# The B and C terms of a selective scan: multiplied on other engines, the B term in place in PSUM

## What is computed

```python
A = -jnp.exp(A_log)
BandC = x @ W_bc.T + b_bc
Bm, Cm = (BandC[..., :n], BandC[..., n:])
delta = jax.nn.softplus(s1 @ W_d.T + b_d)
deltaA = jnp.exp(jnp.einsum('bld,dn->bldn', delta, A))
deltaB_u = jnp.einsum('bld,bln,bld->bldn', delta, Bm, x)
def step(h, inp):
    dA_i, dBu_i, c_i = inp
    h = dA_i * h + dBu_i
    y = jnp.einsum('bdn,bn->bd', h, c_i)
    return (h, y)
```

## Time and profile before

| what | us |
|---|---|
| median of three runs | 6350.38 |
| span of the profiled execution, first to last instruction | 6356.3 |
| TensorE matmul busy | 4749.8 (75%) |
| VectorE busy | 4716.0 (74%) |
| GpSimd busy | 3798.1 (60%) |
| ScalarE busy | 2523.2 (40%) |
| mean granted TensorE clock | 0.837 of full |

### The profile page before, as it was taken

The page is one execution under the profiler, slowest core; times in us unless marked ns, Lnnn a source line. Parts: engine busy times, 40 slices in busy tenths (PEclk is TensorE's granted clock), DMA queues, the critical chain, the costliest instruction groups (busy, mean ns, idle before and its releaser), DMA issues. The chain is left out here.

```text
span 6356.3 us, 78277 instructions
## 1 busy us (share of the span) xinstructions
PE 4749.8 (75%) x24156; PEld 3749.7 (59%) x24156; DVE 4716.0 (74%) x6611; ACT 2523.2 (40%) x4450; POOL 3798.1 (60%) x1772
## 2 busy tenths in 40 slices
PE   3557777777777777777777777777777888887887
PEld 3335555555555555555555555555567777777777
DVE  3899999889999998999899898999733333333333
ACT  2555445555554455555445555554301111111110
POOL 1876666667666666666666666666425555555554
PEclk7578888888788888888888888888988889888888
DMA  2000000000000000000000000000025555555554
GB/s 51 9 22 18 18 20 26 18 18 26 18 18 19 26 19 18 18 26 18 18 20 26 18 18 26 18 10 12 16 70 123 129 124 132 123 130 123 126 128 107
DMA packets 150308, 302.51 MB, mean 48 GB/s; under 512 B 22288, under 2 KB 97492, under 8 KB 149960
## 3 DMA queue, kind: packets, MB, share of 16 engines
q1 hardware_dynamic: 98680, 227.16, 12.7%
q0 software_dynamic: 49152, 69.84, 6.2%
q10 hardware_dynamic: 2128, 1.26, 0.1%
HBM read 236.39 MB, written 61.80 MB: 47 GB/s over the span
## 5 line engine op out<-in xcount | busy, mean ns | idle before, releaser
L476 POOL TENSOR_TENSOR state<-du,b_wide 128x972 f32<-128x972 f32 x512 | 1826.1, 3567 | 463.9 <-ACT b_wide L513 301.5
L610 DVE TENSOR_TENSOR_SCAN state<-decay,state 128x972 f32<-128x972 f32 x512 | 1718.6, 3357 | 81.6 <-POOL state L476 63.3
L486 POOL TENSOR_TENSOR y<-y,state 128x972 f32<-128x972 f32 x448 | 1063.3, 2373 | 962.2 <-DVE state L616 962.2
L513 ACT ACTIVATE b_wide<-ps 128x972 f32<-128x972 f32 x512 | 500.1, 977 | 1120.8 <-PE ps L785 1118.2
L774 PE MATMUL ps<-x2f,ws_u 128*116 128x324 f32 x1024 | 470.7, 547 | 432.5 <-DVE ag L759 431.6
L1072 PE MATMUL e_ps<-xgt,w_up 96*116 96x192 f32 x4096 | 734.4, 333 | 23.7 <-DVE e_ag L1045 23.5
L807 PE MATMUL ps<-ws_d,inter 116*98 116x192 f32 (+1 forms) x3072 | 642.5, 371 | 126.9 <-DVE h L621 124.7
L1072 PEld LDWEIGHTS e_ps<-xgt,w_up 96*116 96x116 f32 x4096 | 680.6, 184 | 27.7 <-DVE e_ag L1045 26.2
L807 PEld LDWEIGHTS ps<-ws_d,inter 116*98 116x98 f32 (+1 forms) x3072 | 585.2, 203 | 160.3 <-DVE h L621 140.2
L1030 DVE TENSOR_TENSOR passed<-counts,tk 96x648 f32<-96x648 f32 x128 | 106.2, 830 | 753.3 <-DMA counts<-running_counts,row_idx 753.3
L983 POOL DMA_INDIRECT xg<-token_rows,gather_idx x256 | 244.8, 956 | 644.0 <-DVE gather_idx L1041 594.5
(11 more groups left out here) (170 smaller groups left out, 8485.2 us busy)
## 6 DMA issues: line engine op xcount, KB each, us to landing
w_up<-in_we_up SPq DMA_DIRECT2D x128, 696.8 KB
w_down<-in_we_down SPq DMA_DIRECT2D x128, 348.0 KB
x_in<-in_x SPq DMA_DIRECT2D x32, 1176.0 KB, 5.3
running_counts<-cnt SPq DMA_DIRECT2D x32, 324.0 KB, 3.3
token_rows<-x SPq DMA_DIRECT2D x64, 148.5 KB
out_rows<-h SPq DMA_DIRECT2D x64, 147.0 KB
token_rows<-x SPq DMA_DIRECT2D x32, 194.0 KB
h<-in_txt SPq DMA_DIRECT2D x32, 192.0 KB, 2.6
```

The lines of the kernel that those rows point to most:

```text
L476: nc.gpsimd.tensor_tensor(b.state[n % 4][:], b.du[t.p][:], b.b_wide[n % 2][:], ALU.mult).then_inc(input_ready, 1)
L486: nc.gpsimd.tensor_tensor(y, y, b.state[n % 4][:], ALU.add).then_inc(y_added, 1)
L513: nc.scalar.activation(b.b_wide[k % 2][:].rearrange("p a t -> p (a t)"), flat[:, b_bank:b_bank + 3 * L], ACT.Copy).then_inc(b_copied, 1)
L610: nc.vector.tensor_tensor_scan(s, b.decay[k % 2][:].rearrange("p a t -> p (a t)"), s, 0.0, ALU.mult, ALU.add).then_inc(scan_done, 1)
```

## The change

B and C swap their ways. **B:** VectorE multiplies the B broadcast with `du` in place in PSUM (piece `fill_b`), and the scan reads its input there and writes `state`. **C:** ScalarE copies the C broadcast to SBUF (`c_wide`, in the place of `b_wide`), and GpSimd multiplies the state with it in place. GpSimd's add is a piece of its own, `add_y`. TensorE may refill `b_bank` once the scan before has ended (`scan_done`) in place of ScalarE's copy (`b_copied`), and `c_bank` once ScalarE has copied (`c_copied`) in place of VectorE's product (`c_used`). The wait that frees one of the four `state` tiles (`y_added`) goes from GpSimd to the scan. The positions of the pieces are new. B is no longer filled two states ahead, but just before its scan.

```diff
--- before.py
+++ after.py
...
 
@@ -74,14 +64,13 @@
 
     for n in range(N):
 
-        b, lag = 2 * (n - 2) + 1, 0
-        if b < 0:
-            b, lag = b + 32, -1
-        put("fill_b", lag, n, pe=b, act=b + 1, pool=b + 2)
+        b, lag = (2 * n - 1.1, 0) if n else (30.9, -1)
+        put("fill_b", lag, n, pe=b, dve=b + 0.9)
         d, lag = (2 * n - 1.5, 0) if n else (30.5, -1)
         put("decay", lag, n, act=d + 0.3)
         put("scan", 0, n, dve=2 * n)
-        put("fill_c", 0, n, pe=2 * n, dve=2 * n + 1.2, pool=2 * n + 2)
+        put("fill_c", 0, n, pe=2 * n - 0.4, act=2 * n + 0.5, pool=2 * n + 1.8)
+        put("add_y", 0, n, pool=2 * n + 2.7)
     for k in range(3):
...
                 for kind, lag, n in todo:
                     t = i.plus(-lag)
-                    if kind == "fill_b":
-
-                        if n == 0:
-                            pool.wait_ge(du_ready, t.v + 1)
-                        pool.wait_ge(b_copied, N * t.v + n + 1)
-                        wait(pool, y_added, 15 * t.v + (max(n - 4, 1) if n >= 4 else n - 3))
-                        nc.gpsimd.tensor_tensor(b.state[n % 4][:], b.du[t.p][:], b.b_wide[n % 2][:], ALU.mult).then_inc(input_ready, 1)
-                    elif kind == "fill_c" and n > 0:
+                    if kind == "fill_c":
+                        pool.wait_ge(c_copied, N * t.v + n + 1)
+                        pool.wait_ge(scan_done, N * t.v + n + 1)
+                        nc.gpsimd.tensor_tensor(b.state[n % 4][:], b.state[n % 4][:], b.c_wide[n % 2][:], ALU.mult).then_inc(c_used, 1)
+                    elif kind == "add_y" and n > 0:
 
                         pool.wait_ge(c_used, N * t.v + n + 1)
                         y = b.y[t.p][:]
@@ -507,10 +493,10 @@
                         to = b.decay[k % 2]
                         nc.scalar.activation(to[:, 0:2, 1:L], b.delta[t.p][:, 0:2, 1:L], ACT.Exp, scale=b.a_neg[:, 0, k:k + 1])
                         nc.scalar.activation(to[:, 2, 1:L], b.delta[t.p][:, 2, 1:L], ACT.Exp, scale=b.a_neg[:, 1, k:k + 1]).then_inc(decay_ready, 1)
-                    elif kind == "fill_b":
-                        act.wait_ge(b_full, N * t.v + k + 1)
-                        wait(act, input_ready, N * t.v + k - 1)
-                        nc.scalar.activation(b.b_wide[k % 2][:].rearrange("p a t -> p (a t)"), flat[:, b_bank:b_bank + 3 * L], ACT.Copy).then_inc(b_copied, 1)
+                    elif kind == "fill_c":
+                        act.wait_ge(c_full, N * t.v + k + 1)
+                        wait(act, c_used, N * t.v + k - 1)
+                        nc.scalar.activation(b.c_wide[k % 2][:].rearrange("p a t -> p (a t)"), flat[:, c_bank:c_bank + 3 * L], ACT.Copy).then_inc(c_copied, 1)
                     elif kind == "emb_a":
 
                         act.wait_ge(x_loaded, 16 * t.v + 16)
@@ -603,17 +589,19 @@
             def body(i, todo, use):
                 for kind, lag, k in todo:
                     t = i.plus(-lag)
-                    if kind == "scan":
+                    if kind == "fill_b":
+                        if k == 0:
+                            dve.wait_ge(du_ready, t.v + 1)
+                        dve.wait_ge(b_full, N * t.v + k + 1)
+                        into = flat[:, b_bank:b_bank + 3 * L]
+                        nc.vector.tensor_tensor(into, into, b.du[t.p][:].rearrange("p a t -> p (a t)"), ALU.mult).then_inc(input_ready, 1)
+                    elif kind == "scan":
                         dve.wait_ge(decay_ready, N * t.v + k + 1)
                         dve.wait_ge(input_ready, N * t.v + k + 1)
+                        wait(dve, y_added, 15 * t.v + (max(k - 4, 1) if k >= 4 else k - 3))
                         s = b.state[k % 4][:].rearrange("p a t -> p (a t)")
-                        nc.vector.tensor_tensor_scan(s, b.decay[k % 2][:].rearrange("p a t -> p (a t)"), s, 0.0,
+                        nc.vector.tensor_tensor_scan(s, b.decay[k % 2][:].rearrange("p a t -> p (a t)"), flat[:, b_bank:b_bank + 3 * L], 0.0,
                                                      ALU.mult, ALU.add).then_inc(scan_done, 1)
-                    elif kind == "fill_c":
-                        dve.wait_ge(c_full, N * t.v + k + 1)
-                        dve.wait_ge(scan_done, N * t.v + k + 1)
-                        s = b.state[k % 4][:].rearrange("p a t -> p (a t)")
-                        nc.vector.tensor_tensor(s, s, flat[:, c_bank:c_bank + 3 * L], ALU.mult).then_inc(c_used, 1)
                     elif kind == "down":
 
                         dve.wait_ge(sums_full, use(kind, k))
@@ -795,10 +783,10 @@
                     if kind == "fill_b":
                         if k == 0:
                             pe.wait_ge(parts_ready, t.v + 1)
-                        wait(pe, b_copied, N * t.v + k)
+                        wait(pe, scan_done, N * t.v + k)
                         spread(t, k, 0, b_bank).then_inc(b_full, 1)
                     elif kind == "fill_c":
-                        wait(pe, c_used, N * t.v + k)
+                        wait(pe, c_copied, N * t.v + k)
                         spread(t, k, 1, c_bank).then_inc(c_full, 1)
                     elif kind in ("down_a", "down"):
                         pe.wait_ge(inter_ready, 2 * NJ * (t.v + 1))
```

More of the change, by code:

```diff
@@ L229, in __init__ @@
         self.decay = two("decay", [128, 3, L])
-        self.b_wide = two("b_wide", [128, 3, L])
+        self.c_wide = two("c_wide", [128, 3, L])
         self.state = two("state", [128, 3, L], n=4)
@@ L403, in phase1 @@
     decay_ready, scan_done = sem("decay_ready"), sem("scan_done")
-    b_full, b_copied, input_ready = sem("b_full"), sem("b_copied"), sem("input_ready")
-    c_full, c_used, y_added = sem("c_full"), sem("c_used"), sem("y_added")
+    b_full, input_ready = sem("b_full"), sem("input_ready")
+    c_full, c_copied, c_used, y_added = sem("c_full"), sem("c_copied"), sem("c_used"), sem("y_added")
     resid_done = sem("resid_done")
```

## The result

The changed kernel takes 6471.24 us in the median (6463.03 to 6489.35, four runs), beside 6346.98 us for the kernel before: a ratio of 1.0203, with a 95% interval of 1.0182 to 1.0223. It is 2.0% slower. I had forecast 5970 us, 6.0% faster. The profiled execution took 6463.03 us.

A forecast was written before the change was run, and what follows sets the result against it. VectorE, busy 91% of the sweep, was taken as the bound. 6356.3 - 577 - 63 + 17 + 115 + 61 + 67 = 5976 us profiled, so 5970 us in the median; forecast 5870 to 6060 us, wider range 5770 to 6160 us.

The forecast's parts named there:

- Step 1: VectorE's scan, reading its input from PSUM, stops waiting for GpSimd and takes 2.23 us: 577 us less.
- Step 2: On VectorE the product with du, writing PSUM, replaces the product with C at the same 1160 ns: 0.
- Step 4: GpSimd's product and add stay, off the path, and ScalarE makes the same number of copies: both 0.
- Step 5: Hand-over of B banks: VectorE waits for TensorE's refill in six of 16 slots, 0.6 us each: 115 us more.
- Step 6: Where VectorE waits for other engines' chains, shorter scans cover less: 61 us more at one place, 67 us elsewhere.
- Step 3: Scan no longer waits for GpSimd's product, 63 us less; it waits for VectorE's product in front, 17 us more.
- The rival "slower": Each B bank hand-over is exposed through TensorE's list, 1.7 us of stall per scan: 6597 us; chance 0.06.

The follow-up runs named there:

- e2: Kernel before with GpSimd's product and adds cut to one element, semaphores kept, for times only: 5283.27 us, 0.8339 of before.
- e4: Changed kernel with one more wait: GpSimd's product of state n starts only when VectorE's product for state n+1 has ended: 5855.0 us.
- e10: Changed kernel with GpSimd's product of state n held until VectorE's product for state n+1 starts: 5556.19 us, 0.8771 of before.
- e1: Changed kernel with GpSimd's product and add cut to one element, semaphores kept, for times only: 5484.79 us, 0.8657 of before.
- e3: Changed kernel with the B broadcast 0.4 positions earlier in TensorE's list: 6835.14 us, 1.0789 of before.
- e5: Changed kernel with the added wait of e4 and the B broadcast 0.3 positions later in TensorE's list: 6120.54 us.
- e6: Changed kernel with only the B broadcast 0.3 positions later in TensorE's list: 6645.27 us, from a single execution.

## Why the prediction was wrong

**Step 1, the scan, was right.** 577 us forecast; 602 us measured over the sweep. The floor of 2.23 us was 0.05 too high.

**Step 2 was right.** The product writes PSUM in place at 1173 ns, 13 ns above the old one, 7 us in all. The scan with its input in PSUM has a median of 2178 ns, and in e2, with both inputs in SBUF and no lock, 2175. The 65 ns per PSUM reader that I had estimated from the Trainium skill (VectorE: DVE Perf Modes, "The TRN2 errata — SBUF-src ops pay a fixed extra latency per instruction") are not there.

**Step 4 is the one that failed.** "GpSimd. Product and add stay ... It is off the path ... Both **0**." I had priced the lock on the scan alone, though my own rows showed two engines that shut each other out, and took all other VectorE lines at their old durations. GpSimd's work stayed, 72 us per pair, and had to fall on something. In the kernel before 19.0 us of its cost per pair fell on the scan and 16.7 on other lines; in the changed one 29.8 fall on other lines, instructions of 0.2 to 1 us. Over the whole sweep the other lines went from 523 to 900 us of lengthening, 377 us for which I had put 0. e4 takes 611 of these 900 us away by one wait, and e10 800; with e10 the kernel ends 414 us below my forecast, which had left the old 523 us where they were. I had no rival for it. L688 and L699, already at 3033 and 3030 ns in the mean in the kernel before with a shortest of 1160 and 1170, were the rows that could have told me, and L643, L644 and L717 are what was hit anew.

**Step 5 was too small.** The wait for the broadcast is 164.5 us against 115. It is not spread over the six tight slots at 0.6 us each: 90 us stand before the product of state 5, one of the six, and 37 before that of state 2, which I had not counted. The 1.26 us at the most that I allowed were a ladder step. The longest wait stands before the product of state 5, in the changed kernel:

```profile
2701.52 2.04 PE L838 MATMUL ps<-ones,x_sq 128*98 128x2 f32 x12
...
2703.43 4.18 PE L842 MATMUL ps<-w_tok,x_in 128*98 128x194 f32 x12
...
2707.40 0.48 PE L770 MATMUL ps<-parts,pick 96*128 96x324 bf16 x1
...
2708.45 1.18 DVE L597 TENSOR_TENSOR ps<-ps,du 128x972 f32<-128x972 f32 x1 [4.24 <-PE ps L773]
```

TensorE has the embedding's matmuls (L838, L842) in front of the broadcast, and VectorE waits 4.24 us. Busy times and the clock of that stretch:

```profile
core 0: us, PE busy (x) PEld busy (x) DVE busy (x) ACT busy (x) POOL busy (x), PEclk, DMA share, GB/s
2701.00:2708.00 7.00, 7.00 (x32) 6.30 (x31) 3.17 (x6) 0.00 (x0) 4.48 (x2) 0.50 0.28 77
```

TensorE was busy for all of the 7.00 us at a granted clock of 0.50, which is 1.2 GHz. With the same lists e4 has 1.5 us per pair at this place and e10 0.2, where the changed kernel has 2.8, so the order alone does not make it.

**Step 6 was right in size, half of it by luck.** The waits for tanh rise by 142.5 us and those for `up_u` fall by 14.9, together 128 as forecast (61 + 67). The place of the earlier trace rows came out as described, an idle time of 0.77 us that was to become 2.7:

```profile
2751.89 0.49 DVE L747 SCALAR_TENSOR_TENSOR ag<-th,ps 116x324 f32<-116x324 f32 x1 [2.44 <-ACT th L575]
```

Over the sweep this ladder step has 49 us more, against 61. The other 67 us were a quarter of all ladder waits; what came are 85 us at a single other step, the one that e1 has as well and e2 has not. That I had not foreseen. A wait for the step size that I had left out rises from 8.4 (`DVE L698`, before) to 48.6 us.

**Step 3.** 35.5 us for the scan behind its product, against 17; and 512 x 0.03 us is 15, not 17.

**The sum.** My sum gave a span of 5976 us, and the profiled execution has 6461.2, 485 us more. By the table the miss divides into 377 us of lengthening on the other lines (step 4), 126 of idle time (323 against 197 for steps 3, 5 and 6 with the 63 us that went), 20 of own work and, the other way, 25 on the scan and 13 behind the sweep. Of the 126, 50 are the broadcast, 40 the step size and 18 the scan behind its product. The 377 us are shown by e1, e4 and e10; the others have only their rows. The rival "slower" had the right sign by another mechanism: it put everything on the hand-over and needed 1.2 us of stall per scan, where the wait for the broadcast is 0.32 us (164.5 / 512) and all that e1 has over e2 is 202 us.

## What to carry to other kernels

A lock between two engines isn't removed by freeing its largest victim: here 602 us left the scan and 377 came back on other instructions. Count the time the other engine holds it, and say which instructions it will meet instead. Where one engine has stretches that need no lock (PSUM operands), hold the other back with a semaphore until they begin: here that turned 2.0% slower into 12.3% faster, with the work unchanged. And when pieces of two in-order lists are tied to each other, small moves can cost more than the change is worth, so try the position on both sides before the change is judged.

## What the runs showed that I had not expected

- A VectorE instruction of 0.17 us takes 2.13 us in the median when it meets GpSimd (L717), as much lost as on an instruction of 0.96 us. What the lock costs here depends on the holder and not on the length of the victim.
- Without GpSimd's work the kernel before takes 17% less time and the changed one 15% less. For the kernel before that is 1056 us (6339 against 5283), beside a lengthening of 608 us on its scans and 523 us on its other lines.
- The granted TensorE clock is 0.83 between 600 and 3900 us, a stretch of the sweep, in the kernel before and in the changed one, and 0.94 in the same stretch of e10. In that stretch TensorE is busy for 2495.2 us in the kernel before, 2438.4 in the changed one and 2699.6 in e10. So part of the gain of e10 may be the clock. VectorE's own work is the same in e4 and e10 (2928 and 2929 us) at 0.88 and 0.94 in this stretch, so the clock could reach it only through its idle time, which is 115 us less; how much of that is the clock no run here shows.
- Moving the B broadcasts by 0.3 or 0.4 of the 32 positions of a pair's list cost 170 to 370 us (e3, e5, e6).
